# Moving the causal mask's products and one transposition in the issue order of a fused attention and feed-forward kernel

## The reference, cut to what matters

```python
x = L0_attn_x                                  # 4 x 1024 x 128
x = x + 0.5 * ffn(layernorm(x))                # hidden size 384
x = x + attn(layernorm(x))                     # 16 heads of 64
x = x + 0.5 * ffn(layernorm(x))

def attn(x):
    q, k, v = x @ wq.T, x @ wk.T, x @ wv.T     # per head; q and k get rotary embedding
    scores = where(causal, q @ k.T * 64 ** -0.5, -inf)
    return concat_heads(softmax(scores) @ v) @ wo.T
```

## Time and profile before

| | |
|---|---|
| median of 3 runs | 1354.47 us (1351.78 to 1355.27) |
| the profiled execution's own time | 1352.74 us |
| its span, first to last instruction | 1351.0 us |
| mean granted TensorE clock | 0.977 |
| PE busy | 1287.3 us (95%) |
| DVE, ACT, POOL busy | 871.9, 618.4, 752.1 us |
| share of DMA queue q1 (SyncE, ScalarE) | 47.6% of 16 engines |

### The profile page before, as it was taken

How to read it: one execution, slowest core, us unless ns; L and a number is a source line. 1 busy time by engine, 2 the same in 40 slices (tenths; PEclk the granted TensorE clock), 3 DMA queues, 4 the chain that set the end, 5 groups by cost and what they waited for, 6 DMA issues and landing times. The chain is left out here.

```text
span 1351.0 us, 24951 instructions
## 1 busy us (share of the span) xinstructions
PE 1287.3 (95%) x6240; PEld 735.7 (54%) x6240; DVE 871.9 (65%) x2270; ACT 618.4 (46%) x1176; POOL 752.1 (56%) x454
## 2 busy tenths in 40 slices
PE   5987599999999999999999999999999999999798
PEld 2544355555555555556555656555555555555365
DVE  5566556677676767676767676767676767664254
ACT  3664134444444444444444444444444444444474
POOL 4134155666565656566666666666666666665300
PEclk9998679999999999999999999999999999999799
DMA  7022546565555556464646464646464646452001
GB/s 275 38 93 87 143 118 159 119 157 121 146 130 131 145 120 156 111 163 113 157 115 161 105 161 108 162 107 162 107 162 105 162 108 162 107 119 52 0 24 39
DMA packets 113612, 165.86 MB, mean 123 GB/s; under 512 B 13360, under 2 KB 63408, under 8 KB 113456
## 3 DMA queue, kind: packets, MB, share of 16 engines
q1 hardware_dynamic: 112784, 163.96, 47.6%
q10 hardware_dynamic: 800, 1.57, 0.6%
HBM read 37.29 MB, written 10.49 MB: 35 GB/s over the span
## 5 line engine op out<-in xcount | busy, mean ns | idle before, releaser
L916 POOL TENSOR_TENSOR psum_p<-psum_p,shared_a 128x256 f32<-128x256 f32 (+1 forms) x192 | 280.8, 1462 | 93.2 <-ACT shared_a L718 83.7
L718 ACT ACTIVATE shared_a<-bank 128x512 f32<-128x512 f32 (+3 forms) x512 | 201.5, 445 | 253.3 <-PE bank L577 251.1
L560 PE MATMUL bank<-k_hh,q_hl 128*128 128x512 f32 (+3 forms) x768 | 258.0, 390 | 15.9 <-DMA k_hh<-parts 10.1
L577 PE MATMUL bank<-q_hm,k_l 65*128 65x512 f32 (+3 forms) x768 | 244.7, 373 | 0.0
L799 DVE TENSOR_REDUCE max_left<-bank 128x1 f32<-128x512 f32 x256 | 175.7, 688 | 101.1 <-PE bank L560 100.9
L560 PEld LDWEIGHTS bank<-k_hh,q_hl 128*128 128x128 f32 x768 | 138.3, 193 | 179.0 <-issue 78.0
L571 PE MATMUL bank<-q_hl,k_hh 128*128 128x512 f32 (+3 forms) x768 | 227.6, 350 | 1.9 <-ACT shared_a L718 1.7
L718 ACT ACTIVATE probs_more<-bank 128x512 f32<-128x512 f32 (+1 forms) x256 | 132.2, 568 | 193.0 <-PE bank L577 175.3
L803 DVE CUSTOM_DVE_ANT_0 max_scratch<-bank,tri_mask,max_left 128x128 f32<-128x128 f32 (+3 forms) x256 | 138.0, 548 | 110.6 <-PE bank L560 110.6
L597 PE MATMUL bank<-shared_a,v_cur 128*64 128x512 f32 (+3 forms) x1024 | 203.0, 475 | 0.0
L894 POOL TENSOR_TENSOR parts<-rotated,parts 128x1024 fp32r<-128x1024 f32 x64 | 152.5, 2383 | 48.4 <-ACT parts L693 48.4
(11 more groups left out here) (127 smaller groups left out, 1916.5 us busy)
## 6 DMA issues: line engine op xcount, KB each, us to landing
q_hl<-parts SPq DMA_DIRECT2D x252, 128.0 KB, 2.8
k_hh<-parts SPq DMA_DIRECT2D x252, 128.0 KB, 2.7
xn_cur<-xn_scratch SPq DMA_DIRECT2D x16, 1024.0 KB, 6.7
v_cur<-shared_b SPq DMA_DIRECT2D x32, 512.0 KB, 6.0
k_l<-parts SPq DMA_DIRECT2D x63, 256.0 KB, 5.2
q_hm<-parts SPq DMA_DIRECT2D x63, 256.0 KB, 5.2
w_qk<-w_scratch SPq DMA_DIRECT2D x32, 256.0 KB, 3.1
w_scratch<-first_w_parts SPq DMA_DIRECT2D x8, 512.0 KB, 3.1
```

The source lines that it names most:

```text
L560: nc.tensor.matmul(max_bank[k % 2][:, 0:w], q_hl[u][h][:, q * P:(q + 1) * P], k_hh[u][h][:, keys * CHUNK:keys * CHUNK + w], start=True, st ...
L577: nc.tensor.matmul(scores[h][:, x0:], k_l1[u][h][:, keys], q_hm[u][h][:, q], start=False, stop=True).then_inc(scores_full, 1)
L718: nc.scalar.activation(probs_of(s)[:, h, x0:], scores[h][:, x0:], ACT.Exp, scale=SCORE_SCALE).then_inc(probs_done, 1)
L916: last = nc.gpsimd.tensor_tensor(acc, acc, new, ALU.add)
```

## The change

In a diagonal step the order was high 0, high 1, mask 0, mask 1, low 0, low 1. Now `score` issues high 0, low 0, high 1, low 1 in every step, and the two masks come later, after the max tiles ahead (and in s = 8 after the output projection) and directly before V's products. They now carry `stop=True` and raise `scores_full`. Unit 25, the transposition of the second half's maxima, goes from its place before V's products of s = 1 to behind them. The first pair keeps its own tiles (`FIRST_MAX`) in their place, but its masks too come behind them. No instruction is added or taken away, and no other engine's code changes.

```diff
-                def with_mask(h):
-                    nc.tensor.matmul(scores[h][:, x0:x0 + P], ident16[:], mask16[:], start=False, stop=False)
-
                 def with_low(h):
-                    nc.tensor.matmul(scores[h][:, x0:], k_l1[u][h][:, keys], q_hm[u][h][:, q], start=False,
+                    return nc.tensor.matmul(scores[h][:, x0:], k_l1[u][h][:, keys], q_hm[u][h][:, q], start=False,
+                                            stop=s not in DIAG)
+
+                for h in range(2):
+                    with_high(h)
+                    last = with_low(h)
+                    if s not in DIAG:
+                        last.then_inc(scores_full, 1)
+
+            def mask_scores(s):
+                x0 = first_col(s)
+                for h in range(2):
+                    nc.tensor.matmul(scores[h][:, x0:x0 + P], ident16[:], mask16[:], start=False,
                                      stop=True).then_inc(scores_full, 1)
-
-                if s in DIAG:
-                    for part in (with_high, with_mask, with_low):
-                        for h in range(2):
-                            part(h)
-                else:
-                    for h in range(2):
-                        with_high(h)
-                        with_low(h)
...
-                    if s == 1 and has_prev:
-                        max_unit(p, i, u, ROWS_UNIT[1])
...
                     if s == 8:
                         project_out(p, i, u, 0)
+                    if s in DIAG:
+                        mask_scores(s)
                     if s >= LAG:
                         times_v(p, u, s - LAG)
...
                     if s == 6:
                         sum_probs(p, 0)
+                    if s == 1 and has_prev:
+                        max_unit(p, i, u, ROWS_UNIT[1])
```

## The result

The changed kernel takes 1366.43 us (median of 4 runs, 1363.46 to 1369.51) against 1354.75 of the kernel before on the same chip. The ratio is 1.0091, 95% interval 1.0064 to 1.0118: slower by 0.9%. The forecast was 1367.5. The profiled execution is the fastest of the four, 1363.46, with a span of 1361.7 and a clock of 0.976.

What follows compares the result with a forecast made beforehand. PE was taken to bound the kernel, busy for all of a 68.80 us double pair. Terms -8.3 + 2.1 + 2.6 + 15.4 + 2 = +13.8, taken as +13 on 1354.5, gave 1367.5 us, range 1349 to 1379.

Steps and rivals of the forecast that it cites:

- Order of the products: Diagonal steps: high, low, high, low covers a late 4-byte weight load in six of eight; -0.26 per pair, -8.3 us.
- V behind the mask: Masks in front of V's products: V ends 1.01 behind the mask as behind other predecessors; zero cost.
- Exponentials later: Step 11's head 1 load waits 0.07 for step 10's later exponentials; +2.1 us, bounds 0 and 0.3 per wait.
- The tile of step 10: Max tile ahead with u = 1 already waits for VectorE, so the step loses 0.17, x 15 = +2.6 us.
- Unit 25, 0.84 and 0.20: Late row delays step 7's exponentials; step 8's head 1 load waits 0.84 (u = 1), 0.20 (u = 0); +15.4 us.
- First pair: Its max tiles, short of VectorE, delay masks and exponentials, with no V in steps 0 and 1; +2 us once.
- The sum: Whole kernel: all terms give +13.8, taken as +13 because small waits may overlap; 1367.5 us.
- slack in the chain: Rival: SyncE's queue copies and their landing absorb the row's 1.13 delay, step 8 doesn't wait; about 1350 us; 10%.
- exponentials in more steps: Rival: PE waits about 0.15 in four more diagonal steps, 19 us on top; 1386 us; 12%.
- a cheaper way to V: Rival: mask to V's products costs less, by 0.1 giving 1341 us, by 0.06 equal to before; 8%.
- no gain from the order: Rival: by the load rule, weight loads are pulled ahead and score order gains nothing; 1375.5 us; 10%.
- two effects that cancel: Rival: unit 25's move stalls but the rest gains more than read, cancelling within 0.3%; 1354 us; 10%.

Runs made afterwards that it cites:

- e7: Kernel before with only SyncE's queue reordered: head 0's four copies go ahead of the row of maxima; 1353.6 us, ratio 0.9993.
- e2: Kernel before with unit 25 alone moved behind V's products of step 1, score products and masks in their old order; 1369.56 us, ratio 1.0122.
- e4: Changed kernel with SyncE's queue reordered: head 0's four copies go ahead of the row of maxima; 1350.26 us, ratio 0.9973.
- e3: Kernel before with only the score order changed: high 0, low 0, high 1, low 1, both masks directly behind, unit 25 in its old place; 1350.9 us, ratio 0.9986.
- e6: e5 with the very first pair's masks directly behind the scores, in front of its max tiles; 1344.26 us, ratio 0.9930.
- e8: Changed kernel with only one of SyncE's copies, instead of four, ahead of the row of maxima; 1353.81 us, ratio 0.9997.
- e1: Changed kernel with unit 25 back in front of V's products of step 1, masks staying at the end of the step; 1351.69 us, ratio 0.9985.
- e5: e4 with step 10's only max tile ahead (unit 18) moved behind V's products; 1347.55 us, ratio 0.9953.
- e9: e6 with step 11's second max tile (unit 21) also moved behind V's products; 1344.33 us, ratio 0.9926.

## Why the prediction was right

- **What bounds the kernel.** Right: what moved on other engines cost or gave nothing until PE waited (e7: L693 1.4 earlier, step 7's exponentials 0.26 earlier, no change).
- **Order of the products, -0.26 per pair.** Right in kind, low in size, and right only together with the place in front of V. The count was off too: two steps are 512 wide and four 384 or 256, so the readings gave 0.28. Measured, the two pairs together gain 0.67, not 0.52. Steps 1 and 3 give 0.04 to 0.055 each once unit 25's share (0.05, e2) is taken off, step 8 0.065 and 0.084 (e4), steps 10 and 11 0.04 to 0.05, step 0 0.02 with u = 1 and 0.10 with u = 0. What I had not seen is that the order alone (e3) keeps this only where no max tile follows the masks. The exposed load of 0.055 in e3's tile says that a load isn't pulled over a mask of 0.06 here. The Trainium skill ("TensorE: Matmul & The Clock Gate", the section on the 32x32 sub-arrays) has TensorE's queue pull weight loads ahead of matmuls in flight; had that reached over the masks, the term would have been zero, and the measured 0.055 says that in this case it does not.
- **V behind the mask, zero.** Right: from the end of the masks to V's end it is 1.01 in the median of step 11 of the kernel after; one of them (timeline, PE):

```profile
867.49 0.29 PE L586 MATMUL bank<-mask,ident 128*128 128x128 bf16 x2
867.70 1.08 PE L597 MATMUL bank<-shared_a,v_cur 128*64 128x512 f32 x4
```

- **Exponentials later, 0.07 in step 11.** The step is right, the head is not, and the size is low with u = 0. Both heads' loads now start 0.05 behind the end of their exponential. The wait that lengthens the step is head 0's, to which I had given none: its product ends 0.13 later with u = 0 (0.409 for 0.282 from end to end) and 0.055 later with u = 1, while head 1's product is not late (0.233 and 0.236). The difference between the pairs is ScalarE's start: step 10's exponentials begin 0.19 behind the first mask with u = 1, as I had read, but 0.26 with u = 0.
- **The tile of step 10, +0.17.** Right: the step is 0.131 longer with u = 1 and 0.059 shorter with u = 0, a difference of 0.19.

```profile
864.78 0.19 PEld L560 LDWEIGHTS bank<-k_hh,q_hl 128*128 128x128 f32 x1 [0.34 <-DVE max_all L805]
865.12 0.12 PEld L586 LDWEIGHTS bank<-mask,ident 128*128 128x128 bf16 x2 [0.16 <-issue]
```

- **Unit 25, 0.84 and 0.20.** Right: against e4, whose TensorE order is the same, step 8 is longer by 0.80 and 0.26. The steps in between were off in ways that cancel. The row is 0.9 later with u = 1, not 1.04, since the negation starts 0.04 behind L555's modelled end, not 0.19. PE reaches step 8 0.155 sooner (the load at 19.157 instead of 19.312 in e4), not 0.09: L555 costs 0.26 behind V but takes over the 0.20 that L530 had paid there (L530 ends 0.118 behind L555, 0.318 behind V before), so its move gained 0.05 that I had left out. In the pairs with u = 0 L693 is 1.12 late, more than the row's 1.0; what adds 0.1 between the last copy's issue and its landing was not tried.
- **First pair, +2.** The place is right. That the two profiles say 2.0 (53.5 against 51.5) is luck: the two groups of traces lie 3.7 apart (e6).
- **The sum.** The terms of the loop gave +0.83 per double pair, 11.6 over fourteen. The medians of the steps give +0.61, because the order gained 0.67 instead of 0.52 and unit 25's place another 0.10; the exponentials cost 0.18 instead of 0.14, the tile 0.18 and step 8 1.06 instead of 1.04. The profile has 10.0 all the same, because the first body is longer by 1.6, most of it in step 8 with u = 0 (4.48 instead of 3.45). So the mechanism was forecast, and that 1366.4 lies so near 1367.5 is in part luck.
- **The rivals.** That of slack in the chain is refuted by e2 and e8 and by the last copy's unchanged 5.4 from issue to landing; that of exponentials in more steps by e1, which shows them in step 11 alone; that of a cheaper way to V by the 1.01 behind the masks; that of no gain from the order by e4's table. That of two effects that cancel didn't come true: the rest gained more than read, but 0.9% stayed.

## What to carry to other kernels

When a product is moved on a saturated engine, follow its result through every queue that waits for it in order, to the first place where the saturated engine waits; here one microsecond passed through VectorE, fourteen DMA issues and four activations, and cost some 15 us (e1, e2), while the rest of the change gained a little in sum (e1). A queue that idles for one item in front of independent ones is a coupling: try to issue the independent ones first, even if that alone gains nothing (e7), since it can keep a later change from costing (e4). The short mask product (0.056) didn't cover the 4-byte load behind it, which was late by 0.05; in front of V's products, which ended 1.01 later in any case, it cost nothing. So look for such a place before moving a short product.

## What the runs showed that I had not expected

- The first L571 of step 0 in pairs with u = 0 takes 0.290 in the kernel before, 0.291 in e2 and 0.286 in e3, but 0.232 in the kernel after and 0.234 in e4, though it is preceded by the same tile. The masks' place differs between these two groups; the cause stays open.
- Waits for VectorE move on by a tile rather than vanish: 0.29 at unit 18 (e4) became 0.15 at unit 21 in every pair (e5), and 0.31 at unit 24 in every second one (e9).
- The transposition between V's products and a projection costs less than between a score and V's: e2's step 1 is 0.05 shorter for the same instructions.
- Step 8 is not longer in the last two pairs (2.66 and 2.03 in the kernel after, 2.73 and 2.22 before): ScalarE has no L695 to run there, so the late row reaches nothing.
